# Six waits moved in a fused attention kernel, and the last pair of probabilities of each chunk summed on TensorE

## The reference

```python
q_hk = (hidden_q @ Wq.T).reshape(Bv, Sv, H, K)
q_big = jnp.einsum('bshk,hkq->bshq', q_hk, w_kc_q)
q_big = _apply_rope(q_big, ...)
kv_r = _apply_rope(kv_c, ...)
q_r = jnp.einsum('bshq,hqr->bhsr', q_big, W_qr)
k_r = jnp.einsum('bld,hdr->bhlr', kv_r, W_kr)
attn = jax.nn.softmax(jnp.einsum('bhsr,bhlr->bhsl', q_r, k_r), axis=-1)
ctx_c = jnp.einsum('bhsl,bld->bhsd', attn, kv_r)
ctx_lat = jnp.einsum('bhsd,hkd->bhsk', ctx_c, w_kc_kv)
out = ctx @ Wo.T                    # x + tanh(g_xattn[1]) * out
```

## Time and profile before

| what | value |
| --- | --- |
| median of 3 runs | 3360.14 us |
| the profiled execution's own time | 3362.52 us |
| its span, first to last instruction | 3360.6 us |
| TensorE busy (matmul) | 2867.2 us, 85% |
| VectorE busy | 2437.6 us, 73% |
| GpSimd busy | 1773.9 us, 53% |
| ScalarE busy | 1485.8 us, 44% |
| mean granted TensorE clock | 0.935 of 2.4 GHz |

### The profile page before, as it was taken

How to read it: one execution, slowest core, us unless ns; L and a number is a source line. 1 busy time by engine, 2 the same in 40 slices (tenths; PEclk the granted TensorE clock), 3 DMA queues, 4 the chain that set the end, 5 groups by cost and what they waited for, 6 DMA issues and landing times. The chain is left out here.

```text
span 3360.6 us, 61691 instructions
## 1 busy us (share of the span) xinstructions
PE 2867.2 (85%) x18352; PEld 1927.7 (57%) x18352; DVE 2437.6 (73%) x4098; ACT 1485.8 (44%) x3074; POOL 1773.9 (53%) x1268
## 2 busy tenths in 40 slices
PE   5999979999788998998998898899899899887345
PEld 4777769999554554564565555455456456554123
DVE  6877755444487787787777778778778777776887
ACT  2333322222155545545545545554554554544456
POOL 0000022222266766757676676776675667664566
PEclk9988879999799999999999999999999999998566
DMA  4000010000300100100000000000000000010100
GB/s 110 0 0 0 0 47 10 10 7 8 79 11 16 25 12 18 23 11 21 18 16 17 20 21 14 19 22 12 19 22 12 20 18 16 11 47 21 57 13 24
DMA packets 130244, 71.05 MB, mean 21 GB/s; under 512 B 83582, under 2 KB 124510, under 8 KB 129880
## 3 DMA queue, kind: packets, MB, share of 16 engines
q1 hardware_dynamic: 129944, 67.45, 8.1%
HBM read 56.95 MB, written 10.04 MB: 20 GB/s over the span
## 5 line engine op out<-in xcount | busy, mean ns | idle before, releaser
L1187 POOL TENSOR_TENSOR c_psum<-c_p 120x800 f32<-120x800 f32 (+1 forms) x384 | 752.5, 1963 | 487.4 <-ACT c_p L1471 277.7
L1471 ACT ACTIVATE c_p<-c_s_ps 120x400 f32<-120x400 f32 (+1 forms) x1536 | 657.2, 507 | 499.8 <-PE c_s_ps L1632 463.1
L1267 DVE TENSOR_REDUCE c_mpart<-c_m_ps 128x1 f32<-128x484 f32 x1080 | 655.8, 652 | 158.5 <-PE c_m_ps L1539 157.0
L1644 PE MATMUL c_o_ps<-c_p,c_val 120*64 120x400 f32 (+1 forms) x3072 | 609.7, 519 | 22.6 <-ACT c_onum L1438 11.4
L1539 PE MATMUL c_m_ps<-c_kmax,c_q 64*128 64x484 f32 x1080 | 324.8, 459 | 116.7 <-DVE c_mpart L1267 112.9
L1294 DVE TENSOR_TENSOR c_acc<-c_acc,c_psum 120x800 f32<-120x800 f32 x256 | 348.7, 1362 | 65.2 <-POOL c_psum L1187 63.1
L1178 POOL TENSOR_TENSOR l_rr<-c_psum,l_rr 96x400 f32<-96x400 f32 x256 | 260.8, 1040 | 192.3 <-DVE l_rr L1316 192.2
L1644 PEld LDWEIGHTS c_o_ps<-c_p,c_val 120*64 120x64 f32 (+1 forms) x3072 | 189.2, 137 | 276.0 <-issue 163.7
L1539 PEld LDWEIGHTS c_m_ps<-c_kmax,c_q 64*128 64x128 f32 x1080 | 144.6, 189 | 341.1 <-DVE c_mpart L1267 273.8
L1575 PE MATMUL c_s_ps<-c_xt,l_a 128*96 128x400 f32 x1536 | 311.2, 352 | 10.6 <-DVE l_rr L1316 8.1
L1628 PE MATMUL c_s_ps<-c_q,c_k 64*120 64x400 f32 (+1 forms) x1536 | 311.6, 369 | 2.6 <-ACT c_p L1471 2.6
(11 more groups left out here) (252 smaller groups left out, 5021.9 us busy)
## 6 DMA issues: line engine op xcount, KB each, us to landing
c_rdb<-l_denominators SPq DMA_DIRECT2D x128, 100.0 KB, 2.7
c_kv<-in_ctx SPq DMA_DIRECT2D x32, 360.0 KB
c_mrow<-c_mneg SPq DMA_DIRECT2D x288, 0.5 KB, 2.0
x_rows<-in_x SPq DMA_DIRECT2D x4, 800.0 KB
x_spill<-x_rows SPq DMA_DIRECT2D x8, 400.0 KB
l_xa<-x_spill SPq DMA_DIRECT2D x8, 400.0 KB
c_xr<-x_spill SPq DMA_DIRECT2D x32, 100.0 KB
x_spill<-c_xr SPq DMA_DIRECT2D x32, 100.0 KB
```

What stands on the lines that cost most here:

```text
L1187: g.tensor_tensor(psum[0:k, u % 2, :], p[0:k, 2 * u % 4, :], p[0:k, (2 * u + 1) % 4, :], ALU.add).then_inc(psum_ready, 1)
L1267: v.tensor_reduce(mpart[:, t, bank:bank + 1], m_ps[:, bank, 0:4 * KP], AX.X, ALU.max, negate=True).then_inc(mpart_ready, 1)
L1471: a.activation(p[0:k, w % 4, i * HALFQ:(i + 1) * HALFQ], s_ps[0:k, (2 * w + i) % 4, 0:HALFQ], ACT.Exp).then_inc(exp_ready, 1)
L1644: mm = pe.matmul(o_ps[i * DL:(i + 1) * DL, 0:HALFQ], val[0:k, j % 2, r, :], p[0:k, w % 4, i * HALFQ:(i + 1) * HALFQ], start=(r == 0), stop ...
```

## The change

Two things are changed, and nothing of what is computed.

1. **The sixth pair.** VectorE no longer adds the pair with q = 5 (`ACC = CP - 2`). `sums` multiplies ones with `acc` (pairs 0 to 4) and then, in the same accumulation, with `psum[1]` (pair 5): four more products of 32 x 200 for each chunk. `psum[1]` is now read by TensorE, so GpSimd's addition with q = 1 of the next chunk, and VectorE's second step in the head, wait for those products (`den_done`); `sums` waits for GpSimd's sixth addition (`psum_ready`).
2. **Six moved steps.** The job "rows" goes from slot 17 to 20, and with it the statistics of the rows, their deviation and their normalisation by two or three pairs. SyncE's `fold_denominators` goes ahead of a `load_combined` (image 1's first chunk; the second chunk of images 0 and 1), and for images 2 and 3 one `load_combined` goes between `fold_denominators` and `write_inverses`. `rotate_keys` steps 0 and 1 go from `at` = 0, 1 of the image before to `at` = 7, 8 of the image before that, and step 2 from `at` = 2 to `at` = 0; for the keys that are rotated in a group's first image nothing moves. The eighth pair of heads is absorbed in bank 2 of `m_ps` instead of `o_ps`.

```diff
-    ACC = CP - 1
+    ACC = CP - 2
...
-            if (j, slot) == (G - 1, 17):
+            if (j, slot) == (G - 1, 20):
                 yield "rows", 0
...
                         load_combined(it, j, 4)
+                        if j == 1:
+                            fold_denominators(b * CH - 1)
                         load_combined(it, j, 5)
-                        if j > 0:
+                        if j > 1:
                             fold_denominators(b * CH - 1)
+                            load_combined(it, j, 6)
                         if j > 0:
                             write_inverses(b * CH - 1)
-                        load_combined(it, j, 6)
+                        if j < 2:
+                            load_combined(it, j, 6)
...
                             load_combined(it, j + 1, 0)
+                        if j < 2:
+                            fold_denominators(b * CH)
+                        if j + 1 < G:
                             load_combined(it, j + 1, 1)
-                        fold_denominators(b * CH)
+                        if j >= 2:
+                            fold_denominators(b * CH)
                         write_inverses(b * CH)
...
+                    if q == 1:
+                        g.wait_ge(den_done, PRIMED + (it * G + j) * CH + c)
...
-                            if at < 3:
+                            if j == 0 and at < 3:
                                 rotate_keys(b + 1, at)
+                            if j > 0 and at == 0:
+                                rotate_keys(b + 1, 2)
...
+                        if (more or j + 2 < G) and j + 1 < G and at in (7, 8):
+                            rotate_keys(b + 2, at - 7)
...
-                        if at == 5 and j + 1 == G and more:
+                        if at == 7 and j + 1 == G and more:
                             deviation(it + 1)
...
                 def head(gi, prev):
-                    if prev:
-                        add_sums(gi * G * CH - 1, CP - 1, gi * NP - 1)
...
+                        if i == 1 and prev:
+                            v.wait_ge(den_done, PRIMED + gi * G * CH)
...
-                                low_queries(it, H // 2 - 1)
-                            if half == 0 and u > 0:
-                                add_sums(ch if q > 0 else ch - 1, (q - 1) % CP, it * NP + u - 1)
+                                low_queries(it, H // 2 - 1, m_ps[:, 2, :])
+                            if half == 0 and q > 1:
+                                add_sums(ch, q - 1, it * NP + u - 1)
...
-                        if more and (j, c, q) == (G - 1, 0, 4):
+                        if more and (j, c, q) == (G - 1, 1, 0):
                             row_stats(it + 1)
-                        if more and (j, c, q) == (G - 1, 1, 0):
+                        if more and (j, c, q) == (G - 1, 1, 2):
                             normalise_rows(it + 1)
...
                         if n == first_in(2, 3 * NC0):
-                            pe.wait_ge(x_added, PRIMED + it * G)
+                            pe.wait_ge(q2_ready, PRIMED + (it + 1) * H)
...
                 def sums(ch):
                     pe.wait_ge(acc_ready, PRIMED + ACC * (ch + 1))
+                    pe.wait_ge(psum_ready, PRIMED + CP * (ch + 1))
+                    k = keys_of(NT - 2)
                     for q in range(4):
-                        mm = pe.matmul(m_ps[q * 32:(q + 1) * 32, 0, 0:QUART], ones[:], acc[:, q * QUART:(q + 1) * QUART], start=True, stop=True)
+                        pe.matmul(m_ps[q * 32:(q + 1) * 32, 0, 0:QUART], ones[:], acc[:, q * QUART:(q + 1) * QUART], start=True, stop=False)
+                    for q in range(4):
+                        mm = pe.matmul(m_ps[q * 32:(q + 1) * 32, 0, 0:QUART], ones[0:k, :], psum[0:k, (CP - 1) % 2, q * QUART:(q + 1) * QUART], start=False, stop=True)
...
                         if r == 0 and (j, c) == (0, 0):
-                            pe.wait_ge(q2_ready, PRIMED + (it + 1) * H)
+                            pe.wait_ge(q2_ready, PRIMED + (it + 1) * H - 2)
...
                             if what == "absorb":
-                                absorbed(it, False, H // 2 - 1)
+                                pe.wait_ge(mpart_ready, PRIMED + it * NMG + issued)
+                                pe.wait_ge(x_added, PRIMED + it * G)
+                                absorbed(it, False, H // 2 - 1, m_ps[:, 2, :])
```

More of the change, by code:

```diff
@@ L1294, in add_sums, with low_queries @@
                         v.tensor_tensor(acc[0:k, :], acc[0:k, :], psum[0:k, q % 2, :], ALU.add).then_inc(acc_ready, 1)
-                def low_queries(gi, pair):
+                def low_queries(gi, pair, src):
                     v.wait_ge(q1_ready, PRIMED + 4 * (gi * (H // 2) + pair + 1))
@@ L1302, in low_queries @@
                         side, at = h // 2 // 4, h // 2 % 4 * S
-                        v.tensor_tensor(q2[side * DL:(side + 1) * DL, :, h % 2, at:at + S], o_ps[rows, 0:T].rearrange("p (b s) -> p b s", b=G),
+                        v.tensor_tensor(q2[side * DL:(side + 1) * DL, :, h % 2, at:at + S], src[rows, 0:T].rearrange("p (b s) -> p b s", b=G),
                                         q1[rows, :, head_cols(2 * pair + half)].bitcast(F32), ALU.subtract).then_inc(q2_ready, 1)
                 def head(gi, prev):
-                    if prev:
-                        add_sums(gi * G * CH - 1, CP - 1, gi * NP - 1)
                     for i in range(H):
@@ L1322, in head @@
                         if i >= 3 and i % 2 == 1:
-                            low_queries(gi, i // 2 - 1)
+                            low_queries(gi, i // 2 - 1, o_ps)
                         if prev and i == 3:
@@ L1371, in _ @@
                 group(NG - 1, False)
-                add_sums(B * CH - 1, CP - 1, NG * NP - 1)
                 done = [0]
@@ L1407, in _, with copy_queries @@
             def _(a):
-                def copy_queries(gi, pair):
+                def copy_queries(gi, pair, src):
                     a.wait_ge(q_ps_ready, PRIMED + gi * (H // 2) + pair + 1)
@@ L1413, in copy_queries @@
                             a.activation(q1[half * DL:(half + 1) * DL, :, head_cols(2 * pair + i)],
-                                         o_ps[i * DL:(i + 1) * DL, 0:T].rearrange("p (b s) -> p b s", b=G), ACT.Copy).then_inc(q1_ready, 1)
+                                         src[i * DL:(i + 1) * DL, 0:T].rearrange("p (b s) -> p b s", b=G), ACT.Copy).then_inc(q1_ready, 1)
                 def copy_keys(b):
@@ L1448, in head @@
                         if i >= 3 and i % 2 == 1:
-                            copy_queries(gi, i // 2 - 1)
+                            copy_queries(gi, i // 2 - 1, o_ps)
                         what, *at = beside_head(i)
@@ L1480, in group @@
                                 if what == "absorb":
-                                    copy_queries(it, H // 2 - 1)
+                                    copy_queries(it, H // 2 - 1, m_ps[:, 2, :])
                                 if what == "den":
@@ L1552, in project, with absorbed @@
                     mm.then_inc(f_ready, 1)
-                def absorbed(gi, prev, pair):
+                def absorbed(gi, prev, pair, dst):
                     n = gi * (H // 2) + pair
@@ L1564, in absorbed @@
                             i = 2 * pair + half
-                            mm = pe.matmul(o_ps[half * DL:(half + 1) * DL, 0:T], m.mqk[:, a, HEADS[i], :], rot[:, i % 4, a, :], start=(a == 0), stop=(a == 1))
+                            mm = pe.matmul(dst[half * DL:(half + 1) * DL, 0:T], m.mqk[:, a, HEADS[i], :], rot[:, i % 4, a, :], start=(a == 0), stop=(a == 1))
                     mm.then_inc(q_ps_ready, 1)
@@ L1582, in head @@
                         if i >= 3 and i % 2 == 1:
-                            absorbed(gi, prev, i // 2 - 1)
+                            absorbed(gi, prev, i // 2 - 1, o_ps)
                         what, *at = beside_head(i)
```

## The result

The changed kernel takes 3325.51 us (median of 4 runs, 3320.32 to 3328.85) against 3363.58 for the kernel before on the same chip: ratio 0.9886, 95% interval 0.9847 to 0.9925. It is 38 us faster; the forecast was 65 faster, 3295. The time lies in the range for 8 in 10 (3245 to 3350), and half a microsecond outside the forecast's own range (3265 to 3325).

What follows compares the result with a forecast made beforehand. TensorE was taken as held by VectorE's amount of work and by steps late on other engines' lists. Gains of 130.0 us less 30.1, 7.0 and 27.6 left 65.3: 3295 us, own range 3265 to 3325, 8 in 10 3245 to 3350.

Steps and rivals of the forecast that it cites:

- A: VectorE's reciprocal no longer waits for the denominators' transfer, in three places per group: 48.6 us gained in all.
- E: The stretch at 1.2 GHz right behind the 3.43 us gap in image 0 goes: 13.1 us gained.
- H: Rotation steps 0 and 1 in 23 second chunks block one VectorE addition per chunk: 27.6 us lost.
- third rival: Second chunks: GpSimd overfilled, its pairs and the exponentials come late; slower, 3422 us at the upper bound; chance 0.09.
- B: First chunks of images 1 and 2: gaps from rotations between the additions go, 34.2 us gained.
- C: Image 3: TensorE's gaps of 1.22 and 1.70 us, with GpSimd late from three rotation steps, go: 20.4 us gained.
- D: VectorE's 64 sixth additions go, and with them TensorE gaps of 1.71 us per group: 13.7 us gained.
- F: A second set of ones products on TensorE's path, 64 times 0.47 us: 30.1 us lost.
- G: Eighth pair in `m_ps`: the gap ahead of the first bank-2 unit stays, two units come behind it: 7.0 us lost.

Runs made afterwards that it cites:

- e2: Kernel before with only the sixth pair moved to ones products on TensorE, no step moved: 3388.91 us, ratio 1.0073.
- e4: Changed kernel with the three rotation steps at the first three pairs of each image again: 3352.11 us, ratio 0.9967.
- e5: Changed kernel with SyncE's list in the order of before: 3363.20 us, ratio 1.0007.
- e12: e11 with the rotation of image 2's keys put back to image 1's first chunk, so image 0's second chunk holds none: 3266.39 us, ratio 0.9703.
- e1: Changed kernel with the sixth pair added by VectorE again, the six moved steps kept: 3313.11 us, ratio 0.9858.
- e6: Changed kernel with the sixth pair's ones products done twice, a third set of four: 3336.84 us, ratio 0.9930.
- e8: e2 plus one wait: in image 3's first chunk GpSimd's first addition waits for VectorE's product c_ct: 3363.44 us, ratio 1.0003.
- e3: Changed kernel with the eighth pair of heads absorbed in `o_ps` again: 3313.02 us, ratio 0.9846.
- e7: Changed kernel with the edits of e1 and e3 together: 3304.24 us, ratio 0.9825.
- e10: e3 plus a wait: in both chunks of image 3 GpSimd's first addition waits for VectorE's product c_ct: 3311.54 us, ratio 0.9849.
- e11: e10 with rotation steps 0 and 1 both behind GpSimd's second addition of the second chunk: 3291.45 us, ratio 0.9792.
- e9: e7 with rotation steps 0 and 1 both behind GpSimd's second addition of the second chunk: 3308.22 us, ratio 0.9830.

## Why the prediction was right in sign and too large

The chunk lengths tell it in one table (mean us over the seven groups that have a next one, from the first scores of each chunk; j.c is image.chunk). Each row is one profiled execution, which lies within 6 us of its kernel's median, that of e5 13 below it.

| | 0.0 | 0.1 | 1.0 | 1.1 | 2.0 | 2.1 | 3.0 | 3.1 | head |
| --- | --- | --- | --- | --- | --- | --- | --- | --- | --- |
| before | 25.3 | 28.9 | 26.2 | 30.6 | 27.1 | 25.5 | 22.7 | 25.1 | 61.8 |
| e2, ones products alone | 25.3 | 28.1 | 25.9 | 29.9 | 28.3 | 25.1 | 25.5 | 26.4 | 61.9 |
| e4, no rotation moved | 27.4 | 22.6 | 25.4 | 30.1 | 28.0 | 25.1 | 26.7 | 25.3 | 61.9 |
| e5, SyncE's list as before | 26.8 | 29.9 | 25.2 | 32.1 | 23.7 | 28.5 | 19.6 | 23.7 | 61.9 |
| changed kernel | 26.7 | 27.2 | 25.1 | 30.5 | 22.5 | 28.5 | 20.8 | 23.7 | 61.8 |
| e12 | 25.0 | 22.6 | 25.4 | 30.8 | 22.4 | 25.7 | 22.4 | 23.7 | 61.8 |

- **A and E, the transfer and the clock behind it.** Right where nothing else fills the chunk: 0.1 goes from 28.9 to 22.6 in e4, 6.3 for 3.43 + 1.6 forecast, and its clock is 1.00. In 1.0 e4 shows 0.9 for the 1.02 forecast, in 1.1 only 0.5 for 1.63: there the prediction had read VectorE's wait, and no row showed a gap of TensorE behind it. In the changed kernel A and E are worth 37.7 (e5), not 61.7: the waits are gone as forecast, and in 0.1 blocked additions take the place of the gap. E came in part: of the 29.9 us that 0.1 had at the 1.2 GHz level in these seven groups, 15.2 are left, but 0.0 rose from 6.6 to 19.0 and 2.1 from none to 17.1. In all images it was 68 us before, 70 after, 37 in e12.
- **H, the rotations in second chunks: the step that failed.** I priced one blocked addition, 1.20 us, per second chunk, and added it to A as if the two were independent, though A takes out the idle time in which the steps could stand. The changed kernel against e4 shows 4.6 in 0.1, 0.4 in 1.1 and 3.4 in 2.1: 8.4 us per group, about 64 in all, not 27.6. In 0.1 the two steps block two additions, and a third is blocked under GpSimd's low keys (3.12 us). With the transfer late and the same steps in it (e5) that chunk is only 1.0 longer than before, though it has more time at the 1.2 GHz level (47.8 us against 29.9). This is the place of the third rival. Its size there, 4.6 us, is over the 4.0 from which I had it cancel the gain, but in one second chunk of three. Its sum was also kinder than the rows: they give 29.13 - 3.43 - 1.6 = 24.1 us for the chunk, not 24.6, for GpSimd's 24.7. Measured were 24.64 us of GpSimd in 27.64.
- **B and C.** Against e4 they came out larger than their upper bounds (together 61): 5.5 in 2.0, 0.3 in 1.0, and in image 3 5.9 and 1.5, so 13.2 per group, about 98 in all. But e4 has the lost order of e2, which the kernel before has not: its 3.0 is 26.7 against 22.7 before. Against the kernel before, the same four chunks shortened by 8.9, and A, B and C forecast 8.2 for them. So B and C were sized about right, and what e4 adds is mostly a price that rotations in first chunks have only when the sixth addition is gone. B + C - H was forecast at 27.0 and measured at 26.6; that these meet is luck, the balance of two terms that each differ by a factor of about 2.
- **D and F.** Forecast -16.4, measured -12.4 (e1). But F is 11.3 at this kernel's margin (e6), under its lower bound of 15, not 30.1; and what D brought is then about zero, if e6's set stands for the second. To count nothing for GpSimd's new freedom at a chunk's first addition was wrong on the kernel before (25.5 us, e8). Its new wait for the products was rightly counted as nothing there: e8 has it.
- **G.** Forecast -7.0, measured -12.5 (e3) and -8.9 (e7): the gap doesn't stay, it grows by 0.71 us, and in 0.0 the time at the 1.2 GHz level is 19.0 us in the seven groups, 5.7 in e3. It isn't the moved absorption alone that brings such time there: e10, without it, has 20.1.
- **The sum.** 37.7 + 26.6 - 12.4 - 12.5 = 39.4 for 38 measured; the moved job "rows" was not undone alone, and that single undoings add up is not certain within their intervals. Term by term, 24 of the missing 27 us are at A and E: what the removed wait gave, the moved rotations took in the same chunk. Taking them out of 0.1 alone brings back 25.1 (e12 against e11), though on a base that has other edits too.

The rule of the Trainium skill ("SBUF — State Buffer", section "SBUF: two separate sides") that the loser waits for the whole instruction is what the timelines show; it speaks of one instruction, and here a VectorE operation was kept out over two in a row (4.02 us over 1.87 and 1.79). By that rule alone blocks only move with the rotations. Here they cost 4.6 us in 0.1, 0.4 in 1.1 and 3.4 in 2.1. That the cost depends on the idle time that the chunk has left fits 0.1 (1.0 with the transfer's wait in e5, 4.6 without it); for the other two it is not shown.

What stays open: why the time at the 1.2 GHz level fell in e11 and rose in e9, and what the moved job "rows" is worth.

## What to carry to other kernels

Before work is moved into a stretch, take that stretch's idle time *after* the wait that the same change removes: image 0's second chunk had room for two steps only as long as the transfer held it up. A wait that seems idle may be what keeps two engines from each other's way, so when a dependency goes, look for what its engine now starts beside. And where a net gain is the balance of two large terms, run each alone: the fastest kernel here keeps the moves that pay and leaves out the one chunk in which they don't.

## What the hardware showed unexpectedly

- Adding a wait on GpSimd made a kernel 25.5 us faster (3388.91 to 3363.44). In its profile the product near the start of image 3 takes 0.56 us; without the wait it took 4.0 in seven of eight groups.
- VectorE's work can be kept out over two GpSimd instructions that follow each other without a pause: 3.12 and 4.02 us for operations of 0.98 and 0.56.
- A gap of 1.91 us is followed by a stretch of 3.41 us at a granted clock of 0.50, just as the gap of 3.43 was the earlier trace rows. With one gap split into three, image 0's second chunk kept half of its time at the 1.2 GHz level (29.9 to 15.2 us in seven groups), and the other chunks together gained as much.
- A third set of ones products, of a kind that moves TensorE's list by 0.45 us, cost 0.18 us of run time.
